# Memory of lines on one core: the blend in the next tile, the decay of the state on ScalarE, tails ahead of the last lines

## The reference, cut to what matters

```python
w1 = (x_prev @ w1w.T).reshape(B, T, H, 4);  w2 = (x @ w2w.T).reshape(B, T, H, 4)
write_lines = exterior(w1, w2)              # 6 products of pairs, divided by their norm
read_lines = exterior(r1, r2)               # the same for r1 and r2
Jw = einsum('bthi,ij->bhtj', write_lines, _J6)
outer = Jw[..., :, None] * Jw[..., None, :]                 # 6 x 6 for each token and head
M_cumsum = cumsum(outer * decay_inv, axis=2), shifted by one token
M_all = M_cumsum * decay_fwd                                # a decayed sum over earlier tokens
rd_M = einsum('bhti,bhtij->bhtj', rd, M_all)
score_M = sum(rd_M * rd);  score_M2 = sum(rd_M * rd_M)
mem_score = (1 - alpha) * score_M + alpha * score_M2
gated = mean(sigmoid(mem_score * mem_scale) * gate)
return (seq_out + gated * mem_val) @ out_w.T + out_b
```

## Time and profile before

| | us |
|---|---|
| median of three runs | 1923.04 |
| the profiled execution | 1920.56 |
| its span | 1918.7 |
| PE busy, of the span | 1854.8 (97%) |
| DVE busy | 1604.3 (84%) |
| ACT busy | 1491.2 (78%) |
| POOL busy | 921.1 (48%) |
| the tiles of the memory of lines | 1149 to 1243 |

### The profile page before, as it was taken

One profiled execution on the slowest core, in us unless ns is written; L12 is line 12 of the kernel. 1 busy time (PEld: TensorE's weight loads), 2 busy tenths in 40 slices (PEclk: granted clock), 3 DMA queues, 4 the chain that ended last, 5 costly groups with the idle time before them and its releaser, 6 DMA issues. The chain is left out here.

```text
span 1918.7 us, 61287 instructions
## 1 busy us (share of the span) xinstructions
PE 1854.8 (97%) x22646; PEld 1108.4 (58%) x22646; DVE 1604.3 (84%) x5459; ACT 1491.2 (78%) x4110; POOL 921.1 (48%) x552
## 2 busy tenths in 40 slices
PE   7999999999999989999999998889999999999999
PEld 3777774577775443433443447637777635777754
DVE  6899974899995669999999949979999658999945
ACT  5999994699998362777777763469999947999973
POOL 2788860488882050000000035548888505888820
PEclk9999999999999996999999999999999999999999
DMA  6212130122221041111111000002121201221311
GB/s 183 47 44 51 44 70 6 29 50 46 49 54 40 1 153 37 42 42 42 42 42 42 25 6 4 2 20 51 44 51 44 62 6 36 47 48 45 68 23 44
DMA packets 76331, 85.33 MB, mean 44 GB/s; under 512 B 17328, under 2 KB 50804, under 8 KB 75908
## 3 DMA queue, kind: packets, MB, share of 16 engines
q1 hardware_dynamic: 75839, 81.40, 17.0%
q10 hardware_dynamic: 196, 0.02, 0.0%
HBM read 20.83 MB, written 8.39 MB: 15 GB/s over the span
## 5 line engine op out<-in xcount | busy, mean ns | idle before, releaser
L336 ACT ACTIVATE probs<-probs,negmax 128x128 f32<-128x128 f32 x1024 | 402.0, 402 | 1.5 <-DVE negmax L411 1.0
L2334 ACT ACTIVATE gprobs<-ps_global 128x1024 f32<-128x1024 f32 (+3 forms) x384 | 291.4, 811 | 124.7 <-PE ps_global L1765 102.1
L291 POOL TENSOR_TENSOR rot<-rot 128x1024 f32<-128x1024 f32 x128 | 302.5, 2364 | 142.6 <-DVE rot L381 142.6
L297 POOL TENSOR_TENSOR qk<-rot,cnorm 128x1024 f32<-128x1024 f32 x128 | 243.9, 1906 | 172.8 <-issue 149.1
L304 POOL TENSOR_TENSOR probs<-probs,iden 128x1024 f32<-128x1024 f32 x128 | 242.9, 1898 | 46.6 <-DVE iden L419 46.0
L2010 DVE TENSOR_REDUCE maxes<-ps_global 128x1 f32<-128x512 f32 (+2 forms) x384 | 221.9, 637 | 10.4 <-PE ps_global L1728 6.5
L411 DVE CUSTOM_DVE_ANT_0 probs<-ps_attn,masks 128x128 f32<-128x128 f32 x1024 | 226.1, 284 | 0.6 <-issue 0.5
L336 ACT ACTIVATION_READ_ACCUMULATOR probs<-probs,negmax 128x1 f32 x1024 | 204.6, 200 | 0.0
L1723 PE MATMUL ps_global<-kq 48*128 48x512 bf16 (+3 forms) x768 | 196.8, 345 | 7.3 <-DVE maxes L2010 1.8
L2251 POOL CAST m_parts<-m_turn 32x128 bf16<-32x128 f32 x16 | 4.5, 279 | 363.7 <-DVE m_turn L2024 363.7
L377 DVE TENSOR_TENSOR rot<-ps_attn,rotary 128x512 f32<-128x512 f32 x256 | 174.7, 682 | 2.0 <-PE ps_attn L202 1.6
(11 more groups left out here) (235 smaller groups left out, 4490.8 us busy)
## 6 DMA issues: line engine op xcount, KB each, us to landing
v_first<-v_second SPq DMA_DIRECT2D x256, 128.0 KB, 2.3
hs<-z_a SPq DMA_DIRECT2D x256, 32.0 KB, 1.9
ln<-z_b SPq DMA_DIRECT2D x56, 128.0 KB, 2.4
kq<-split_scratch SPq DMA_DIRECT2D x64, 96.0 KB
kq<-split_scratch SPq DMA_DIRECT2D x64, 64.0 KB
split_scratch<-parts SPq DMA_DIRECT2D x8, 384.0 KB, 4.4
split_scratch<-gprobs SPq DMA_DIRECT2D x6, 384.0 KB, 4.0
x_tok<-in_x_dram SPq DMA_DIRECT2D x4, 512.0 KB, 5.9
```

The costliest lines, as they stand in the source:

```text
L291: nc.gpsimd.tensor_tensor(a, a, b, ALU.add).then_inc(C["rot_sum"], 1)
L297: nc.gpsimd.tensor_tensor(qk[:, k % 2, :].rearrange("p (h d) -> p h d", d=DH), rot_a[:, k % 2, :, :], cnorm[:, k % 2, :].unsqueeze(2).to_b ...
L336: last = nc.scalar.activation(probs[:, k % 2, slot, :], probs[:, k % 2, slot, :], ACT.Exp, scale=-1.0, bias=negmax[:, k % 2, slot:slot + 1 ...
L2334: nc.scalar.activation(probs[:, step % RING, 2 * p:2 * p + 2, 0:w], ps[:, S0 + 2 * p:S0 + 2 * p + 2, 0:w], ACT.Exp).then_inc(C["p2_exp"], 1)
```

## The change

On DVE, `advance` for all tiles but the first adds the tail to an already decayed copy of the state in two operations, in place of four that decay and add. On ACT the new `fade` makes that decayed copy, `faded`, in four operations, for the states 1 to 6, behind `copy_scores`. On DVE, `multiply` of lines 6 and 7 moves ahead of the second half of `read_memory`; `sum_squares` of w = 0 moves behind it; `sum_squares` of w = 1 moves behind `advance`; and `clip` of w = 1 moves into the next tile, behind its first `terms`. On ACT the copies of lines 0 and 1 move from the start of a tile to the tile before, between `square_line` of w = 1 and its `inverse`, and the copies 6 and 7 move ahead of `square_line` of w = 0. On PE, `tails` moves ahead of the last part of `memory`. POOL's list is as it was.

```diff
@@ -1558,7 +1558,7 @@
             "o_out0", "o_out1", "qk_in0", "qk_in1", "qk_in2", "m_in0", "m_in1", "m_in2", "later_in"))
     C.open(("ml_set", "ml_proj", "ml_left", "ml_mul", "ml_line", "ml_square", "ml_ssq", "ml_log", "ml_inv", "ml_clip", "ml_unit",
             "ml_outer", "ml_tail", "ml_state", "ml_row0", "ml_row1", "ml_m", "ml_term", "ml_read", "ml_plain", "ml_blend", "ml_weight",
-            "ml_score", "ml_turned", "ml_out"))
+            "ml_score", "ml_turned", "ml_out", "ml_faded"))
     U2 = P2_STEPS
     QK_DMAS, M_DMAS, O_DMAS = 4 * len(JOINED), 2 * PARTS, GROUP + 1
     with ExitStack() as ctx:
@@ -1583,6 +1583,7 @@
         rstd = o_cols
         later = sb("later", [P, CHUNK])
         den_late = sb("den_late", [P, 2 * CHUNK // AH])
+        faded = sb("faded", [P, GROUPS, B * LINE * LINE])
         ps = ctx.enter_context(nc.psum_tensor(C.own("ps_global"), [P, 8, CHUNK], F32))
         S0, O0, M0 = 0, 4, 5
 
@@ -1903,9 +1904,9 @@
                     inverse_and_mean(0)
                 memories(3, 5)
                 lines(4, 6)
-                memories(5, 6)
                 if t + 1 < LAST:
                     tails(t + 1)
+                memories(5, 6)
                 lines(6, 8)
                 if valid(t - 1):
                     turn(t - 1)
@@ -2080,6 +2081,15 @@
                 if k == 0:
                     wait(dve, "ml_set", 1)
                 wait(dve, f"ml_row{(k + 1) % 2}", 16 * ((k + 1) // 2))
+                if k > 0:
+                    wait(dve, "ml_faded", k)
+                    for half in range(2):
+                        at = slice(half * GROUPS // 2, (half + 1) * GROUPS // 2)
+                        last = nc.vector.tensor_tensor(state[:, (k + 1) % 2, at, :].rearrange("p q n -> p (q n)"),
+                                                       faded[:, at, :].rearrange("p q n -> p (q n)"),
+                                                       ps[:, TAIL_BANKS[half], 0:2 * STATE_ROWS], ALU.add)
+                    last.then_inc(C["ml_state"], 1)
+                    return
                 for q in range(GROUPS):
                     last = nc.vector.scalar_tensor_tensor(out=state[:, (k + 1) % 2, q, :], in0=state[:, k % 2, q, :],
                                                           scalar=A["whole"][:, q:q + 1], in1=tail_of(k, q), op0=ALU.mult, op1=ALU.add)
@@ -2138,6 +2148,8 @@
 
                 multiplies(0, 1)
                 all_terms(0, 1)
+                if 1 < t + 1 < S_TILES:
+                    clip(t + 1, 1)
                 multiplies(1, 2)
                 all_terms(1, 3)
                 multiplies(2, 4)
@@ -2148,20 +2160,19 @@
                 all_terms(4, 5)
                 multiplies(5, 6)
                 all_terms(5, 6)
+                multiplies(6, 8)
+                if valid(t):
+                    read_memory(t, 1)
                 if valid(t + 2):
                     sum_squares(t + 2, 0)
-                if valid(t):
-                    read_memory(t, 1)
-                multiplies(6, 8)
                 if valid(t):
                     weigh(t)
                 if valid(t + 2):
                     clip(t + 2, 0)
-                    sum_squares(t + 2, 1)
                 if t + 1 < LAST:
                     advance(t + 1)
                 if valid(t + 2):
-                    clip(t + 2, 1)
+                    sum_squares(t + 2, 1)
 
             wait(dve, "oo_stage", 1)
             nc.vector.tensor_tensor(A["out_bias"][:, :], ps[:, VALUES, 0:1], A["cols"][:, V_OUT:V_OUT + 1], ALU.add
@@ -2397,6 +2408,12 @@
                                      unit[:, 1, k % 2, :, :].rearrange("p x c -> p (x c)"), ACT.Identity,
                                      scale=A["alpha"][:, 1:2]).then_inc(C["ml_plain"], 1)
 
+            def fade(k):
+                wait(act, "ml_state", k)
+                for q in range(GROUPS):
+                    last = nc.scalar.activation(faded[:, q, :], state[:, k % 2, q, :], ACT.Identity, scale=A["whole"][:, q:q + 1])
+                last.then_inc(C["ml_faded"], 1)
+
             def copy_scores(k):
                 wait(act, "ml_turned", k + 1)
                 nc.scalar.copy(line_scores[:, k * TILE:(k + 1) * TILE], ps[:, TURN, 0:TILE]).then_inc(C["ml_out"], 1)
@@ -2417,24 +2434,27 @@
                                      ).then_inc(C["oo_value"], 1)
 
             def body(t):
-                def lefts(first, end):
+                def lefts(t, first, end):
                     if valid(t + 2):
                         for i in range(first, end):
                             copy_left(t + 2, i // B, i % B)
 
-                lefts(0, 2)
+                if t == 0:
+                    lefts(t, 0, 2)
                 if valid(t - 2):
                     copy_scores(t - 2)
-                lefts(2, 5)
+                if 0 < t + 1 < LAST:
+                    fade(t + 1)
+                lefts(t, 2, 5)
                 if valid(t):
                     scale_lines(t)
-                lefts(5, 6)
+                lefts(t, 5, 8)
                 if valid(t + 2):
                     square_line(t + 2, 0)
-                lefts(6, 8)
-                if valid(t + 2):
                     inverse(t + 2, 0)
                     square_line(t + 2, 1)
+                lefts(t + 1, 0, 2)
+                if valid(t + 2):
                     inverse(t + 2, 1)
 
             square_centred(0)
```

## The result

The changed kernel takes 1934.92 us (median of four runs, 1932.85 to 1936.4), the kernel before 1922.55 (also of four): a ratio of 1.006, 95% interval 1.0048 to 1.0072. It is slower by 12.4 us. The forecast was 9.0, and the range held the time. The profiled execution after took 1936.4 us with a span of 1934.6, the slowest of the four, against 1920.56 and 1918.7 before.

The account below looks back on a forecast made before the run. DVE looked like the bound, nearly balanced by a loop through POOL that would decide after the change. First clip +1.3, five periods 7.4, reciprocal +0.35: +9.0 us on the median 1923.04, so 1932.0, range 1926.0 to 1937.0.

Parts of the forecast that it names:

- What bounds it: Lines' tiles: DVE looks like the bound, 12.14 busy of 12.82 us, but a second chain is almost as long.
- The chain through POOL: Clip, normalise, outer_products, PE, ACT's copy, multiply 7, DVE's work, next clip: period 14.3 us, 1.47 more per tile.
- memory 5: Four PE passes at 0.123 us between tails and lines 6 and 7, entering the loop: 0.49 us.
- DVE's own queue: DVE's work per tile falls from 12.82 to about 11.2 us: advance saves 0.38, weigh 0.68, the filled gap 0.55.
- fade: 24 new ACT operations, 1.6 us for four, covered up to 2.9 us: no cost and no gain.
- The ends: First moved clip +1.3 us, clip behind the reciprocal +0.35; after the last clip everything follows as before.
- behind the reciprocal: Behind tile 1 the reciprocal, 0.55 us long, pushes the clip behind its inverse: +0.35 us.
- rival E: PE's clock drops from 2.4 to 1.2 GHz in these tiles, doubling PE's part: +15 us more, 1947; chance 0.03.
- signs of being wrong: A period under 13, tails not waiting for POOL, DVE without gaps, or a granted clock under 1.00 in the stretch.
- B: DVE's queue decides: five tiles at 11.2 us, at most -9.6, 1913.4 us; chance 0.08.
- C: Pieces put in series overlap in part: period about 13.4 us, +3 to +5, 1927 us; chance 0.08.
- D: Gain and loss cancel: period near 12.8 us, 1923 us; chance 0.05.

Follow-up runs that it names:

- e1_tails_back: The changed kernel with tails put back behind memory 5 on PE, the rest as changed; 1931.52 us, ratio 1.0043 to the kernel before.
- e3_orders_back: The changed kernel with PE's tails, DVE's sum_squares and read_memory, and ACT's square_line put back in their old orders; 1925.93 us, ratio 1.0017 to the kernel before.
- e1_clip_back: The changed kernel with clip of w=1 put back straight behind sum_squares of w=1 on DVE; 1938.22 us, ratio 1.008 to the kernel before.
- e2_filler: The changed kernel with useless matrix products added on PE ahead of line 2 and tails, tiles 1 to 5; 1930.78 us, ratio 1.0045 to the kernel before.

## Why the prediction was right, and where its sizes were off

**What bounds it.** Right. DVE looked like the bound and a second loop of nearly the same length decided: DVE has 4.0 us less to do in five periods and they take 8.65 us more.

**The chain through POOL.** Right step by step, counted from the clip: tails at 5.18 (5.16 in the forecast), multiply 7 at 8.72 (8.59), sum_squares of w = 1 at 13.10 (12.95), the next clip at 14.44 (14.29). The term that was too small is memory 5: it takes 0.60 of PE's queue behind tails (1201.22 to 1201.82), not 0.49, since I took the four passes at the price of ten in a row. Five times 0.14 is 0.7 us. e1_tails_back and e3_orders_back show the loop by taking steps out of it, e1_clip_back by moving one that costs the period nothing. tails wait 1.22 us for outer_products (1.4 in the forecast).

**DVE's own queue.** advance 0.73 (0.72), weigh's multiply 0.56 (0.56), both as forecast. The estimate from the Trainium skill's VectorE: DVE Perf Modes, 0.43 us each, is close to the recorded length of these operations (0.81 for two that overlap) and not to what they take from the queue.

**fade.** Right: 0.31 us from start to start, 1.33 for the four, covered. (By the Trainium skill's ScalarE: Activation LUTs 0.40 each in length; the trace agrees.)

**The ends.** First moved clip +1.40 (+1.3); behind the reciprocal +0.31 (+0.35). In the profiled execution the tiles started 1.34 us late (1149.01 against 1147.67) before any edited instruction had run; 0.86 of that is there by 31 us (ACT's row of line L516 at 31.98 against 31.12). It is no effect of the change.

**The clock, rival E, was mis-sized.** The sum of the forecast has no term for it. I gave it 0.03, and only as a fall in all the tiles at once, +15. A granted clock under 1.00 in the stretch was one of my signs of being wrong, and it came (0.97 over the five periods). Rival E is true in part: in the changed kernel 4.3 us behind the last clip and 0.4 in the tiles. The sum for the profiled execution is 1.34 + 1.40 + 8.65 + 4.26 = 15.65 us up to the next stage, of a span longer by 15.9. e2_filler gives the loop nearly without the clock: 1930.78 less 1922.18 is 8.6 us, against the 9.0 of the forecast. By its profiled execution it is 1.39 at the first clip, 8.24 in the periods and 0.07 behind them, 9.7 us, which is the forecast and the 0.7 of memory 5. The measured 12.4 less 9.7 or 8.6 leaves some 3 to 4 us for the clock, an estimate. Nothing in the sum stood for it: that it took so little, and that the time stayed in the range, was luck in this part. My reason for the low chance was the row of 6.17 busy of 8 us at full clock. A share of busy time was the wrong thing to compare: the tile at 1192.79 has 11.55 busy of 14.43 and a full clock, and the one behind it, with the same waits, has 0.88.

**Rivals B, C and D** are out: no period is under 14.4 in the changed kernel. That a shorter chain would by itself make DVE's queue decide was not so either: with outer_products early and the clip no longer waiting for it the period is still 13.34.

## What to carry to other kernels

When an engine is busy 95% of a steady loop, look for the second loop before shortening its queue: write down the chain from one instruction to itself a tile later, across engines, and see which side of the last arrival an edit puts each piece of work on. Work moved behind the last arrival enters the loop at its full price, however much was saved elsewhere. An order on one engine is tied to those of the others, and also keeps operations apart that would wait for each other.

## What the runs showed of the hardware

- A one-input DVE operation between SBUF tensors (tensor_scalar, 128x64 f32, 0.18 us) waited for a two-input GpSimd operation to end: 3.12 to 3.62 us. A tensor_reduce of 128x128 in the same place took 0.28. Products with one operand in PSUM ran beside it unchanged (0.34, 0.60). The Trainium skill states in GPSIMD Engine Reference, Specifications, that GpSimd shares its SBUF interfaces with VectorE, with contention for DVE instructions with two SBUF inputs or in a 2-port performance mode. The trace fits, though no run shows in which mode the clip ran, and it adds the size: the clip waited until the whole GpSimd instruction of 4.03 us was over (1202.24 against 1202.18, and 1203.89 against 1203.85 in the kernel before with this edit).
- PE's granted clock fell to half behind waits of some 1.5 to 3 us in kernels whose tiles repeat alike, in some tiles and not in others (0.88 and 1.00 in neighbouring tiles), and it cost most in the matmul stretch behind the tiles (4.3 us against 0.4). Filling the waits with products kept it full through the five periods and gave back 4.2 us behind them. Why one tile loses it and the next doesn't stays open.
